# A transformer layer, step by step on five engines: three instructions' places in the order of a step are changed

## The reference, cut to what matters

```
g = x @ Wg.T + bg;  v = x @ Wv.T + bv                    # 16 heads of 8
corr = g.g / (|g| |g|)   in a causal window of 128, then (corr + 1) / 2
denom = mean(corr over keys) + 0.5
fit   = 1 / (denom * sum over tokens(1 / denom))         # per head
P     = softmax(corr * fit, masked);  out = P @ v
y1 = layernorm(x + out @ Wo.T + bo)                      # "first norm"
xq = fp4(y1): blocks of 16, scale = max|.| / 6, rounded to a small grid
h  = silu(xq @ w_gate.T) * (xq @ w_up.T);  hq = fp4(h)
result = layernorm(y1 + hq @ w_down.T)                   # "second norm"
```

## Time and profile before

| | |
|---|---|
| median of 3 runs | 336.33 us |
| the profiled execution, whole | 335.8 us |
| its span, first to last instruction | 333.8 us |
| busy share of the span: PE, DVE, ACT, POOL | 79%, 76%, 64%, 59% |
| mean granted TensorE clock | 0.955 of full |

### The profile page before, as it was taken

The page is one execution under the profiler, slowest core; times in us unless marked ns, Lnnn a source line. Parts: engine busy times, 40 slices in busy tenths (PEclk is TensorE's granted clock), DMA queues, the critical chain, the costliest instruction groups (busy, mean ns, idle before and its releaser), DMA issues. The chain is left out here.

```text
span 333.8 us, 12978 instructions
## 1 busy us (share of the span) xinstructions
PE 264.9 (79%) x5044; PEld 177.6 (53%) x5044; DVE 253.2 (76%) x697; ACT 213.0 (64%) x515; POOL 198.6 (59%) x471
## 2 busy tenths in 40 slices
PE   5515778989798998989898989998989999635541
PEld 3313344655466665757575666666656665514330
DVE  5723369476989898989898899999888897836631
ACT  2101535586869787877878787978788896433231
POOL 6363545346485778686869686777873553442541
PEclk9999999999999999999999999999999999975855
DMA  4032112122123313340522233223312100010000
GB/s 120 16 63 50 32 33 49 36 49 51 33 50 35 60 24 84 29 86 20 81 34 65 45 57 40 61 66 34 51 33 60 26 20 18 0 32 2 16 16 21
DMA packets 42884, 14.19 MB, mean 43 GB/s; under 512 B 35586, under 2 KB 42820, under 8 KB 42820
## 3 DMA queue, kind: packets, MB, share of 16 engines
q1 hardware_dynamic: 42820, 13.33, 20.8%
HBM read 2.84 MB, written 2.10 MB: 15 GB/s over the span
## 5 line engine op out<-in xcount | busy, mean ns | idle before, releaser
L596 ACT ACTIVATE Pm<-S 128x384 f32<-128x384 f32 x256 | 112.2, 495 | 51.4 <-PE S L788 51.2
L809 PE MATMUL OT<-Pm,gv 128*32 128x256 f32 (+1 forms) x1024 | 58.3, 348 | 0.0
L782 PE MATMUL S<-BT,AT 32*32 32x160 f16 (+4 forms) x2048 | 41.0, 224 | 16.9 <-ACT Pm L596 10.6
L511 POOL TENSOR_TENSOR hq<-hm,hs 128x352 f32<-128x352 f32 x32 | 24.9, 795 | 36.8 <-DVE hm L1234 36.8
L782 PEld LDWEIGHTS S<-BT,AT 32*32 32x32 f16 x2048 | 17.8, 88 | 50.6 <-ACT Pm L596 34.3
L933 PE MATMUL WD<-wdT,hqT 128*128 128x128 f32 (+1 forms) x192 | 29.0, 307 | 14.7 <-ACT hqT L664 14.7
L809 PEld LDWEIGHTS OT<-Pm,gv 128*32 128x32 f32 x1024 | 27.6, 113 | 20.9 <-issue 8.2
L933 PEld LDWEIGHTS WD<-wdT,hqT 128*128 128x128 f32 (+1 forms) x192 | 25.8, 213 | 17.4 <-ACT hqT L664 17.4
L788 PE MATMUL S<-mask,ident 32*32 32x96 f16 x1024 | 31.3, 207 | 0.0
L853 PE MATMUL WA<-wgv,xT 128*128 128x256 f32 x64 | 22.8, 489 | 4.6 <-DMA bgrow<-bg_dram 3.5
L505 POOL TENSOR_TENSOR hn<-h,hrn 128x352 f32<-128x352 f32 x32 | 25.4, 815 | 1.3
(11 more groups left out here) (161 smaller groups left out, 633.6 us busy)
## 6 DMA issues: line engine op xcount, KB each, us to landing
xT<-x_turned_dram SPq DMA_DIRECT2D x16, 128.0 KB, 2.3
out_dram<-yo SPq DMA_DIRECT2D x16, 128.0 KB, 2.1
AT<-A SPq DMA_TRANSPOSE x32, 2.5
BT<-B SPq DMA_TRANSPOSE x32, 2.5
wf<-w_down_dram SPq DMA_DIRECT2D x1, 176.0 KB, 2.4
wgv<-wgv_dram SPq DMA_DIRECT2D x1, 128.0 KB
wf<-w_gate_dram SPq DMA_DIRECT2D x1, 128.0 KB, 2.2
wf<-w_up_dram SPq DMA_DIRECT2D x1, 128.0 KB, 2.1
```

What stands on the lines that cost most here:

```text
L511: pool.tensor_tensor(b3(hq[:, k, 0:I]), b3(hm[:, k]), bc(hs[:, k], QB), ALU.mult).then_inc(s_hq, 1)
L596: act.activation(Pm[:, group % PR, hd % 4, :], S[:, (H * x + hd) % 3, 0:SCW], ACT.Exp, scale=1.0 / ZS).then_inc(s_exp, 1)
L782: pe.matmul(S[k0:k0 + KG, bank, at:at + n], AT[r:r + 32, x % 2, c, q:q + KG], BT[r:r + 32, x % 2, c, q:q + n], start=(kt == 0), stop=False)
L809: i = pe.matmul(OT[VP * g:VP * (g + 1), T - (q1 - q0):T], gv_flat[:, at:at + VP], Pm[:, (GROUPS * x + c) % PR, g, q0:q1], start=(kt == 0 a ...
```

## The change

Three moves; no instruction is added or taken away.

1. **PE.** `fitness_sums(t)` is called inside `project(t)`, behind the passes of x and ahead of the wait for the attention and the passes by Wo. In steps without a projection it stays where it was.
2. **POOL.** The first norm's `rstd` stands ahead of B's high piece, directly behind newton.
3. **DVE.** `low_B` stands behind `h_scale`'s last two instructions in place of ahead of them. The three instructions of `gene_size` stand between those of `round_h`: `n` ahead of the second half's first, the first seed between the two of that half, the second seed behind them. They stood behind both, between the instructions from `gw` to `den`.

```diff
--- before.py
+++ after.py
@@ -530,6 +530,8 @@
 
                 if live(t + 2) and t not in (-2, 0):
                     newton(t + 2)
+                if live(t - 2) and t != B + 1:
+                    rstd(t - 2, mv1, ve1, rstd1, nm1, nb1, s_ln1, 4 * (t - 2) + 4, s_rs1)
                 if live(t + 1):
 
                     pool.wait_ge(s_fit, 7 * (t + 1) + 7)
@@ -537,8 +539,6 @@
                     pool.tensor_copy(B16[:, :, 0:3:2, :], twice(Bf)).then_inc(s_Bhi, 1)
                 if t == 0:
                     newton(2)
-                if live(t - 2) and t != B + 1:
-                    rstd(t - 2, mv1, ve1, rstd1, nm1, nb1, s_ln1, 4 * (t - 2) + 4, s_rs1)
                 if live(t + 2):
 
                     pool.wait_ge(s_gh, t + 3)
@@ -829,6 +829,8 @@
                 for k in range(NT):
                     pe.matmul(WB[:, k * D:(k + 1) * D], xT[:, (t - 1) % XR, k * P:(k + 1) * P], identf[:, :],
                               start=(k == 0), stop=False)
+                if live(t + 2):
+                    fitness_sums(t)
                 pe.wait_ge(s_xac, t)
                 for k in range(NT):
                     pe.matmul(WB[:, k * D:(k + 1) * D], xaT[:, k * P:(k + 1) * P], woT[:, :],
@@ -979,7 +981,7 @@
                 scores(t, 7)
                 if live(t - 1) and t < B:
                     project(t)
-                if live(t + 2) and t != -1:
+                elif live(t + 2) and t != -1:
                     fitness_sums(t)
                 values(t, 2)
 
@@ -1329,11 +1331,11 @@
                         gene_size(1, k)
                 if live(t - 3):
                     h_scale(t - 3, 0)
-                if t >= 1 and live(t + 1):
-                    low_B(t + 1)
                 if live(t - 3):
                     h_scale(t - 3, 1)
                     h_scale(t - 3, 2)
+                if t >= 1 and live(t + 1):
+                    low_B(t + 1)
 
                 if t == B + 1:
                     for step in range(7):
@@ -1386,29 +1388,29 @@
                 if t == B:
                     sums_1(B - 1)
                     aggr_1(B - 1)
+                early_genes = live(t + 3) and t >= 0
+                if early_genes:
+                    gene_size(t + 3, 0)
                 if live(t - 3):
                     round_h(t - 3, 1, 0)
+                if early_genes:
+                    gene_size(t + 3, 1)
                 if live(t - 4) and t != B + 1 and not late(t - 4):
                     aggr_2(t - 4)
                 if live(t - 3):
                     round_h(t - 3, 1, 1)
-
-                early_genes = live(t + 3) and t >= 0
                 if early_genes:
-                    gene_size(t + 3, 0)
+                    gene_size(t + 3, 2)
+
                 if live(t + 2):
 
                     n = 7 * (t + 2)
                     dve.wait_ge(s_win, t + 3)
                     dve.tensor_tensor(gw[:, :, :].rearrange("p h d -> p (h d)"), gh[:, :, :].rearrange("p h d -> p (h d)"),
                                       WB[:, 0:T], ALU.mult).then_inc(s_fit, 1)
-                if early_genes:
-                    gene_size(t + 3, 1)
                 if live(t + 2):
                     dve.wait_ge(s_fit, n + 1)
                     dve.tensor_reduce(rs[:, :], gw[:, :, :], AX.X, ALU.add).then_inc(s_fit, 1)
-                if early_genes:
-                    gene_size(t + 3, 2)
                 if live(t + 2):
                     dve.wait_ge(s_fit, n + 2)
                     dve.tensor_scalar(den[:, :], rs[:, :], 0.5 / T, 1.0, ALU.mult, ALU.add).then_inc(s_fit, 1)
```

## The result

The changed kernel takes 341.81 us (median of 4 runs, 341.42 to 345.06), the kernel before, run beside it, 336.70 us (4 runs, 336.30 to 339.24). The ratio is 1.0145, 95% interval 1.0092 to 1.0198: slower. Applied to the 336.33 us of before, that is 341.2 us. The forecast was 339.1 us; 341.2 lies near the upper end of the forecast's whole range (334.0 to 341.6), and outside the 338.0 to 340.8 that it gave its own mechanism. The profiled execution took 341.42 us, its span is 339.6 us at a mean granted clock of 0.952 (before: 335.8, 333.8, 0.955).

What follows compares the result with a forecast made beforehand. The step (15.87 us) was bound by POOL's leg 1 plus DVE's leg 2. Nine steps by 0.29 make 2.6; with 0.2, 0.3 and -0.3 that is +2.8 us, hence 339.1 us, range 334.0 to 341.6.

Steps and rivals of the forecast that it cites:

- leg 2: DVE's part of a step, from `hn` to the last `hm`: 5.73 us before, forecast 6.06 in steps 3 to 12.
- leg 1: POOL's part of a step, from the last `hm` to `hn`: 10.14 us before, forecast 10.10.
- Seeds, +0.33 a step: DVE, leg 2: `n` ahead of the second half's first `hm` delays the last `hm` by 0.33; first seed taken as free.
- nothing in leg 1 needs `rden` at once: DVE's `rden`: at best 0.5 earlier after the last `hm`, at worst as now, 0.1 taken; no immediate need in leg 1.
- Sums, "Taken as 0, between -0.1 and +0.2": PE: sums ahead of Wo make PE wait for `rden`, costing nothing more since the legs set the step; us a step.
- PE does not close this circle: Premise that only POOL and DVE set the step of 15.87 us, PE needing their results in passing.
- Root and `low_B`, -0.04 in leg 1: POOL: root ahead of B's high piece frees `nb`, but `low_B` then holds `hrn`; leg 1 from 10.14 to 10.10.
- Step 0, +0.3 once: Filling up: both seeds come ahead of `gw`, moving `rden` and PE's sums by 0 to 0.45; 0.3 taken.
- Nine steps, +2.6: Full pipeline: nine steps, each longer by 0.33 - 0.04 = 0.29 us, 2.6 us in all.
- Steps 13 and 14, -0.3: Emptying: no seeds there and `hr` earlier, so 0.3 us less in all.
- every meeting goes against it: Rival: `hs` caught behind A's high piece, `low_B` behind that; leg 1 10.35, step 0.54 longer, 341.4 us; chance 0.15.
- The faster rival: `low_B` stops disturbing POOL; leg 1 near 9.54, step 0.27 shorter, 334.1 us; chance 0.22.

Runs made afterwards that it cites:

- e4: Kernel before with only the seeds moved between the roundings of h: 338.23 us, ratio 1.0040, not distinguishable from before.
- e1: Changed kernel with the three gene_size instructions back behind the roundings of h, other moves kept: 339.01 us, ratio 1.0078.
- e5: Kernel before with the first norm's root ahead of B's high piece and `low_B` behind `hs` and `hr`, no seeds or sums moves: 334.90 us, ratio 0.9956.
- e2: Changed kernel with the sums back behind the projection, other moves kept: 338.45 us, ratio 1.0069.
- e6: Kernel before with only the sums moved between x and the passes by Wo: 339.90 us, ratio 1.0099.
- e10: Kernel before with only `low_B` moved behind `hs` and `hr`: 332.50 us, ratio 0.9882.
- e3: Changed kernel with `den` taken directly from one reduction (factor in `gw`, ninth column of ones): 334.33 us, ratio 0.9926.
- e11: e3 with the sums back behind the projection: 334.00 us, ratio 0.9923.
- e7: Changed kernel with `den` folded into the reduction, `n` ahead of `gw`, both seeds behind `rden`: 337.47 us, ratio 1.0035, not distinguishable from before.
- e8: Kernel before with `den` folded into the reduction, `n` ahead of `gw`, both seeds behind `rden`: 335.71 us, ratio 0.9977, not distinguishable from before.
- e9: Kernel before with only the first norm's root moved ahead of B's high piece: 342.85 us, ratio 1.0209.

## Why the prediction was right, and where not

The sign and the mechanism it named first were right: leg 2 grew by 0.33 in each step (16.26 = 10.20 + 6.06), for the reason given. That leg 1 came out near its forecast was luck: two misses of opposite sign met there. The edits added one by one give an account of a step: 15.86, with `low_B` 15.48, with the root 15.69, with the sums 16.03, with the seeds 16.27. In another order the terms differ: the root costs 0.21 behind `low_B`'s move and 0.67 alone, the seeds 0.24 at the end and nothing alone.

- *Seeds, +0.33 a step.* In leg 2 exact. Alone, the seeds give the 0.33 back in leg 1 (e4), which the prediction did not count; on top of the other edits they cost 0.24 to 0.29 (e1 to after, e5 to e2). The step's words "`den` falls into that same time and inherits the wait" came true: 0.74 in place of 0.17. But "nothing in leg 1 needs `rden` at once" ceased to hold through the sums.
- *Sums, "Taken as 0, between -0.1 and +0.2".* This step failed. It compared `rden` (172.21) with Wo (172.19) for the old DVE order and took the two legs as setting the step whatever PE did. Measured: +0.33 (e6), +0.34 (e5 to e1), +0.29 (e2 to after), above the upper bound. PE's queue carries everything up to `th`, so a wait at its head closes a third way round the step. The premise behind it, "PE does not close this circle", was already doubtful in before: `hr` had about 0.04 to spare there, and in two steps POOL waited for it. The times on PE themselves were read well: Wo stood to be late by the sums' length, and in e6 it starts 3.23 after the last `hm`, against 2.78.
- *Root and `low_B`, -0.04 in leg 1.* Together -0.17 a step (e5); of it `low_B` -0.38 alone and the root +0.21 on top. That `hs` is caught behind a cast came true with the root: behind A's high piece in after (0.38), as the bound had it, but behind B's in e5 (0.60). The interference of `low_B` does move to `hrn`, but costs 0.32 there, not "most of its 0.68". Leg 1's forecast of 10.10 was thus near 10.20 because -0.17 from these was foreseen only as -0.04, and about +0.3 from the sums not at all.
- *Step 0, +0.3 once.* The sums start 46.95 in place of 46.55, +0.40, inside 0 to 0.45. Up to step 3 the shift is +0.43, predicted 0.5; but over the profiled executions of the other kernels this shift runs from 0.02 (e1) to 3.29 (e10), so the +0.2 of step 3 is not shown.
- *Nine steps, +2.6.* Measured +4.70: 3.0 from leg 2, 1.7 from leg 1, of which 1.1 falls in one step, 3 to 4 (10.81 against 9.71), where TensorE ran partly at its lower clock (last section; in e5, without that stretch, leg 1 of this step is 9.95 as in the others). Without that step the error of the sum is about 0.1 a step.
- *Steps 13 and 14, -0.3.* Measured +0.92, nearly all (0.85) in the step from 13 to 14. No seeds stand there, yet `den` lasts 0.82 where it had 0.18 in before, and PE's sums wait 0.45 for `rden`.

Of the rivals, "every meeting goes against it" (341.4) has the nearest time, but not the cause: `hr` is late through `th`, besides `hs` being held. The faster rival is the one that e10 realises (step 15.48, 332.5 us): its mechanism was sound, but only with the root left where it was. That POOL would wait elsewhere than ahead of `hq` was named as a sign of failure, and it does, though the step still is the sum of the two legs.

Left open: how far e3 and e10 add up was not tried, nor the sums ahead of Wo with an early `rden` in a kernel in which POOL does wait for `hr`.

## What to carry to other kernels

Before a consumer is moved ahead on an in-order queue, list everything that stands behind it there and follow that to the loop's closing engine; equal times in the old schedule do not make the move free, as what stands behind may have no room (here about 0.04 us). An engine that shows no wait for a result may still get it only just in time. When several moves come in one change, price each alone and with the others: here one move gained 0.38 a step, and the other three, added in the order above, took 0.8 back between them. An instruction of 0.17 us that lasts 0.74 beside another engine's long one is best taken off the chain, or put into a form that is not held there, as the reduction in e3.

## What was not expected of the hardware

In some executions TensorE's granted clock falls to half for some microseconds in step 3. In after PE waits 1.12 us for `attn` there. The window after it, columns stretch, us, busy us of PE, PEld (weight loads), DVE, ACT, POOL (with counts), granted clock, DMA share, GB/s:

```profile
88.00:92.00 4.00, 4.00 (x31) 2.73 (x30) 3.90 (x11) 2.74 (x7) 0.36 (x2) 0.57 0.10 21
```

The same window of before, where that wait was 0.56:

```profile
88.00:92.00 4.00, 3.52 (x56) 2.01 (x54) 3.86 (x11) 3.31 (x9) 0.77 (x2) 1.00 0.02 4
```

The clock is granted at 0.57 there, a mix of the two levels of 1.2 and 2.4 GHz, against 1.00. The four passes of x by the weights of g and v lasted 1.64 against 1.13. PE of after, 86 to 91 us:

```profile
87.80 1.64 PE L855 MATMUL WA<-wgv,xT 128*128 128x256 f32 x4 [1.12 <-DVE attn L1362]
```

The wait by itself does not explain it. In e5 PE waits 1.13 us at the same place, and the clock stays. PE of e5, 86 to 91 us:

```profile
88.00 1.13 PE L853 MATMUL WA<-wgv,xT 128*128 128x256 f32 x4 [1.13 <-DVE attn L1360]
```

The same window of e5, columns as above:

```profile
88.00:92.00 4.00, 4.00 (x58) 2.87 (x59) 3.86 (x9) 3.84 (x11) 0.73 (x2) 1.00 0.14 30
```

In e11 the clock is at half in the window from 87 to 88 us, while PE still waits for `attn` (until 88.04). What the falls share is that PE did little ahead of them: in after it was busy 2.19 of the 4 us before, in e11 0.40 of the microsecond from 85.5 to 86.5. But in e5 it was busy 2.19 of the same 4 us too.

The profiled executions of e1, e2, e3, e7, e10 and e11 show such a stretch in step 3 too, those of before, e4, e5, e6, e8 and e9 do not. In e4 one lies at 230 to 236 us (granted 0.51) and lengthens that step by 2.5 us; that is the step left out of e4's mean. PE waited 0.79 us for `hqT` ahead of it, but before has the same wait of 0.79 in most steps, without a fall. Why the fall comes in one execution and not in another was not settled.
